# Transformer block on one core: shared-expert blocks reordered around the last second norm and the last router

## What is computed

```python
x = x + tanh(g0) * attention(layernorm(x), ctx)      # scores, softmax, values, output projection
h = layernorm(x)                                     # the second norm
router = h @ gate_w.T                                # 8 experts
top_p, top_i = top_k(softmax(router), 2)             # "ranking": the two best per token
y = sum over the two experts of top_p * ((silu(h @ fc1.T) * (h @ fc2.T)) @ proj.T)
shared = (silu(h @ sfc1.T) * (h @ sfc2.T)) @ sproj.T # 704 hidden units, for all tokens
y = y + sigmoid(h @ shared_gate_w.T) * shared
out = x + tanh(g1) * y
```

## Time and profile before

| | us |
|---|---|
| median of three runs | 304.88 |
| the profiled execution | 305.98 |
| its span, first to last instruction | 304.2 |
| PE busy | 276.9 (91%) |
| DVE busy | 215.7 (71%) |
| ACT busy | 170.6 (56%) |
| POOL busy | 131.1 (43%) |

### The profile page before, as it was taken

One profiled execution on the slowest core, in us unless ns is written; L12 is line 12 of the kernel. 1 busy time (PEld: TensorE's weight loads), 2 busy tenths in 40 slices (PEclk: granted clock), 3 DMA queues, 4 the chain that ended last, 5 costly groups with the idle time before them and its releaser, 6 DMA issues.

```text
span 304.2 us, 5865 instructions
## 1 busy us (share of the span) xinstructions
PE 276.9 (91%) x1785; PEld 249.0 (82%) x1785; DVE 215.7 (71%) x698; ACT 170.6 (56%) x399; POOL 131.1 (43%) x163
## 2 busy tenths in 40 slices
PE   0978989999999789799999999799999999999992
PEld 1867968888788667489888888689999999998891
DVE  2664777879968948766776775877787777863285
ACT  1565676777756546555325455456667666664230
POOL 1350361361587154732333000037777777786000
PEclk9997999999999999999999999999999999999996
DMA  6451107203028031433233665258888888866796
GB/s 196 173 176 69 70 11 239 82 21 122 1 77 280 1 110 53 151 130 120 92 123 128 188 232 185 59 134 139 136 136 138 137 137 143 126 71 69 239 353 239
DMA packets 30510, 40.18 MB, mean 132 GB/s; under 512 B 2960, under 2 KB 26640, under 8 KB 30480
## 3 DMA queue, kind: packets, MB, share of 16 engines
q1 hardware_dynamic: 22336, 29.53, 31.0%
q0 software_dynamic: 7152, 9.57, 19.0%
q10 hardware_dynamic: 992, 0.71, 0.9%
HBM read 22.68 MB, written 17.11 MB: 131 GB/s over the span
## 4 chain that ended last, share of the span: by engine, by line
PE 55%; DVE 23%; ACT 8%; issue 6%; POOL 3%; DMA 3%; DVEq 0%; ACTq 0%; SPq 0%; POOLq 0%
PE bank L415 43%; PE bank L654 6%; DVE ew_lo L1002 4%; ACT ew_hi L769 3%; PE bank L747 3%; DVE work L1332 3%; PE bank L703 3%; DVE xt_lo L1002 2%; ACT sh_hi L769 2%; DMA consts_sb<-consts_dram 2%; DVE work L1354 2%; DVE neg_max L1046 2%; ACT work L801 1%; DVE sh_lo L1002 1%; DMA weight_stage<-ew_dram 1%
## 5 line engine op out<-in xcount | busy, mean ns | idle before, releaser
L1522 POOL DMA_INDIRECT y_d<-work,dest_of_slot x39 | 60.5, 1552 | 56.3 <-DVE dest_of_slot L1378 54.7
L415 PE MATMUL bank<-ew_hi,xt_hi 128*128 (+2 forms) x172 | 53.8, 322 | 1.1 <-DVE xt_lo L1002 0.8
L415 PE MATMUL bank<-ew_lo,xt_hi 128*128 (+2 forms) x172 | 51.9, 302 | 0.0
L415 PE MATMUL bank<-ew_hi,xt_lo 128*128 (+1 forms) x133 | 40.5, 305 | 0.0
L1002 DVE TENSOR_TENSOR xt_lo<-bank,xt_hi 128x256 fp32r<-128x256 f32 (+2 forms) x90 | 35.7, 398 | 3.0 <-ACT xt_hi L769 1.5
L1482 POOL DMA_INDIRECT xs_d<-xn_all,slot_of_pair x32 | 32.0, 1001 | 10.1 <-issue 7.3
L415 PE MATMUL bank<-ew_hi 128*128 128x256 f32 (+1 forms) x100 | 31.5, 321 | 3.9 <-DVE ew_lo L1002 2.0
L1002 DVE TENSOR_TENSOR ew_lo<-bank,ew_hi 128x512 fp32r<-128x512 f32 (+1 forms) x41 | 22.7, 581 | 16.9 <-ACT ew_hi L769 16.8
L769 ACT ACTIVATE xt_hi<-bank 128x256 fp32r<-128x256 f32 (+1 forms) x90 | 32.7, 409 | 3.5 <-PE bank L747 2.2
L415 PE MATMUL bank<-xt_hi,sw_hi 128*128 128x512 f32 x88 | 34.6, 394 | 0.0
L415 PE MATMUL bank<-xt_lo,sw_hi 128*128 128x512 f32 x88 | 34.5, 392 | 0.0
(11 more groups left out here) (159 smaller groups left out, 688.5 us busy)
## 6 DMA issues: line engine op xcount, KB each, us to landing
work<-xs_d SPq DMA_DIRECT2D x39, 136.0 KB, 2.5
weight_stage<-ew_dram SPq DMA_DIRECT2D x10, 486.5 KB, 3.7
ew_hi<-y_d SPq DMA_DIRECT2D x8, 512.0 KB, 7.4
y_d<-work SPq DMA_DIRECT2D x6, 512.0 KB, 3.9
work<-ctx_t_dram SPq DMA_DIRECT2D x4, 512.0 KB, 3.5
xn_all<-x_dram SPq DMA_DIRECT2D x3, 512.0 KB, 6.5
xs_d<-pad_row SPq DMA_DIRECT2D x9, 136.0 KB, 1.8
weight_stage<-sw_dram SPq DMA_DIRECT2D x3, 384.0 KB, 3.2
```

What stands on the lines that cost most here:

```text
L415: last = nc.tensor.matmul(dst, a, b, start=(n == 0), stop=(n == len(pairs) - 1))
L1522: nc.gpsimd.indirect_dma_start(out=y2_d, out_offset=bass.IndirectOffsetOnAxis(ap=IX[:, n:n + 1], axis=0), in_=EY[:, n % 4, :], in_offset=None,
```

## The change

No instruction is added or removed: each engine has the same operations in another order.

- PE: the second half of `fc(0, 0)` goes ahead of `attend(3, 3)`. The first half stays behind it. The first half of `fc(0, 3)` goes ahead of `router(3)` and the second half between `router(3)` and `logits(3)`; before, the whole block stood behind `pj(0, 1)`. `route(3)` moves from behind `fc(0, 5)` to behind `pj(0, 4)`, and the wait for v_keep from behind `fc(1, 0)` to ahead of `fc(1, 1)`. The definition of `fc` moves up, and it gives its semaphore behind the half that is issued last.
- ACT: `second_apply(3, 1)` goes ahead of `s_hi(0, 0)`. Behind `logits(3)` comes `expert_weights(0)`, and then `s_hi(0, 2)`. `route_exp(3)` and the tanh of the shared gate move behind `s_hi(0, 3)`.
- DVE: `shared_tail_lo(1)` goes ahead of `s_lo(0, 0)`. `slots(2)`, `logits(3)` and `shifted(3)` stand behind `s_mult(0, 2)`, with `expert_weights(0)` after them and ahead of `s_lo(0, 2)`. `two_best(3)` goes behind `s_lo(0, 3)`, `counts(3)` behind `s_lo(0, 4)`, `shared_gate` behind `s_lo(0, 5)`.
- SP: the same list. The loads of pieces 0 and 1 still wait for the end of `shared_tail_lo(1)`, which uses the same staging buffer.

```diff
-PIECE_AT = ((0, 3), (0, 4), (1, 3), (1, 4), (1, 5), (2, 1), (2, 1), (2, 2), (2, 3), (2, 4))
+PIECE_AT = ((0, 2), (0, 4), (1, 3), (1, 4), (1, 5), (2, 1), (2, 1), (2, 2), (2, 3), (2, 4))
...
-                if halves[-1] == 1:
+                if halves[-1] == 1 and (s, j) != (0, 0) or (s, j, halves[0]) == (0, 0, 0):
                     last.then_inc(p_fc, 1)
...
                 if c < LAST:
                     project(c + 1, 3)
+                else:
+                    pe.wait_ge(sw_hi, 1)
+                    pe.wait_ge(sw_lo, 1)
+                    fc(0, 0, (1,))
                 attend(c, 3)
...
-            fc(0, 0)
+            fc(0, 0, (0,))
             fc(0, 1)
             route(LAST - 1)
             second_norm(LAST, 0)
             second_norm(LAST, 1)
             fc(0, 2)
+            fc(0, 3, (0,))
             router(LAST)
+            fc(0, 3, (1,))
             logits(LAST)
...
                     if n < len(order):
+                        if order[n] == (1, 0):
+                            route(LAST)
+                        if order[n] == (1, 1):
+                            pe.wait_ge(v_keep, 1)
                         fc(*order[n])
-                        if order[n] == (0, S_BLK - 1):
-                            route(LAST)
-                        if order[n] == (1, 0):
-                            pe.wait_ge(v_keep, 1)
...
             pj(0, 0)
-            blocks(0, PRE, 3)
+            pj(0, 1)
+            blocks(0, PRE, 4)
```

On ACT, in the loop over (s, j):

```diff
                     s_silu(s, j)
+                    if (s, j) == (0, 0):
+                        second_apply(LAST, 1)
+                    if (s, j) == (0, 1):
+                        second_hi(LAST, 0)
+                        second_hi(LAST, 1)
                     if (s, j) == (0, 2):
                         logits(LAST)
+                        expert_weights(0)
...
                     s_hi(s, j)
+                    if (s, j) == (0, 3):
                         route_exp(LAST)
                         act.wait_ge(v_lg, N_CH)
                         nc.scalar.activation(GS[:], LG[:, :, N_E], ACT.Tanh, scale=0.5).then_inc(a_gs, 1)
```

On DVE, in its loop:

```diff
-                    if (s, j) == (0, 2):
-                        logits(LAST)
-                        shifted(LAST)
                     s_mult(s, j)
+                    if (s, j) == (0, 0):
+                        shared_tail_lo(1)
                     if (s, j) == (0, 1):
                         second_lo(LAST, 0)
                         second_lo(LAST, 1)
+                    if (s, j) == (0, 2):
+                        slots(LAST - 1)
+                        logits(LAST)
+                        shifted(LAST)
+                        expert_weights(0)
...
                     s_lo(s, j)
-                    if (s, j) == (0, 0):
-                        slots(LAST - 1)
-                        shared_tail_lo(1)
-                    if (s, j) == (0, 2):
+                    if (s, j) == (0, 3):
                         two_best(LAST)
+                    if (s, j) == (0, 4):
                         counts(LAST)
+                    if (s, j) == (0, 5):
                         shared_gate()
-                    if (s, j) == (0, 5):
                         slots(LAST)
```

More of the change, by code:

```diff
@@ L566, in warm, with fc @@
                     nc.tensor.transpose(B[5][:, 0:P], ident, ident)
+            def fc(s, j, halves=(0, 1)):
+                for i in halves[:2 if j < S_FULL else 1]:
+                    last = chain(B[pair(s, j) + i][:],
+                                 [(SFC[a][:, k, 2 * j + i, :], XT[b][:, s, k, :]) for k in range(KD) for a, b in THREE],
+                                 [(0, v_h, 6 * s + j - 1)] if i == 0 else ())
+                if halves[-1] == 1 and (s, j) != (0, 0) or (s, j, halves[0]) == (0, 0, 0):
+                    last.then_inc(p_fc, 1)
             pe.wait_ge(d_const, 16)
@@ L624, in _ @@
                     project(c + 1, 3)
+                else:
+                    pe.wait_ge(sw_hi, 1)
+                    pe.wait_ge(sw_lo, 1)
+                    fc(0, 0, (1,))
                 attend(c, 3)
[L627 to L632, removed]
-                if halves[-1] == 1:
-                    last.then_inc(p_fc, 1)
             def pj(s, j):
@@ L965, in _ @@
                     s_silu(s, j)
+                    if (s, j) == (0, 0):
[3 more added lines that the diff above has]
+                        second_hi(LAST, 1)
                     if (s, j) == (0, 2):
                         logits(LAST)
+                        expert_weights(0)
+                    if (s, j) == (PRE - 1, S_FULL):
+                        e_step(-2, 2, -1)
+                    s_hi(s, j)
+                    if (s, j) == (0, 3):
                         route_exp(LAST)
@@ L970, in _ @@
                         nc.scalar.activation(GS[:], LG[:, :, N_E], ACT.Tanh, scale=0.5).then_inc(a_gs, 1)
[L971 to L976, removed]
-                    if (s, j) == (0, 0):
-                        second_apply(LAST, 1)
-                    for n in range(E_PIECES):
+                    for n in range(1, E_PIECES):
                         if PIECE_AT[n] == (s, j):
```

## The result

The changed kernel takes 301.65 us (median of 16 runs, 299.95 to 303.14), the kernel before in the same comparison 304.43 us (16 runs, 302.56 to 306.48). The ratio is 0.9898, 95% interval 0.9878 to 0.9918: faster by 2.8 us, about three times the 0.9 us that a measurement tells from no change. Forecast were 301.7 us and a gain of 3.2. That the time itself is met within 0.05 is luck: the gain is 0.4 smaller, and the kernel before took 0.45 less in this comparison than the 304.88 from which the forecast started.

What follows compares the result with a forecast made beforehand. The prediction took PE to bound the kernel, with DVE close behind. Filled waits gave 3.8 us at pj(0, 2), less 0.6 given back by DVE: a gain of 3.2, so 301.7 us, range 300.8 to 303.9.

Steps and rivals of the forecast that it cites:

- Step 1: PE, half of fc(0, 0) ahead of attend(3, 3): gain 1.38 us, hidden by a wait of 1.5; nothing held.
- Step 2: PE at second_norm(3, 1): the 1.26 us wait goes, as second_apply ends at 120.2; 0.10 is waited at route(2).
- Step 3: PE ahead of fc(0, 2): a new wait of 0.48 us for s_mult(0, 0) on DVE, bounds 0.3 and 0.7.
- Steps 4 and 5: PE at router(3) and logits(3): waits of 0.92 and 0.84 us go, with 0.45 and 0.4 to spare.
- Step 6: ACT's expert_weights(0) ahead of s_hi(0, 2), and pj(0, 2) directly behind pj(0, 1): costs nothing, up to 0.3 us.
- The sum: At pj(0, 2) on PE: 1.38 + 1.26 + 0.92 + 0.84 less 0.10 less 0.48, 3.8 us gained.
- Step 7: DVE up to s_mult(1, 0): counts(3) and the shared gate give back 0.6 us, bounds 0 and 1.25; 3.2 holds.
- Step 8: Exp and table loads behind s_hi(0, 3), then two_best ahead of s_mult(0, 4): costs nothing, with 0.4 us to spare.
- DVE holds more: Rival: late DVE blocks and the moved counts and gate cut the gain to 1.0 to 2.1 us; chance 0.17.
- Nothing is kept: Rival: expert weights, tables and scatters have a time of their own, so the time is 304.9 us; chance 0.09.
- the loop slows: Rival: expert loop steps take 0.09 us more, eating the 3.2, or 0.13 more, giving 306.5 us; chance 0.08.
- More is gained: Rival: counts and gate fall wholly into idle time and s_mult(0, 0) follows the attention, gain 3.9 to 4.2; chance 0.06.

Runs made afterwards that it cites:

- the last version: Changed kernel with counts(3) and shared gate in DVE's idle gaps and s_mult(0, 0) ahead of shared_tail_lo(0): 299.86 us, and 301.48 us on another chip.

## Why the prediction was right

- *Step 1* held exactly: the attention product's third matmul starts at 112.12, aligned 115.09, for the 115.10 of the earlier trace rows, and the next block where it was. Nothing is held.
- *Step 2*: the table load stands at 114.32, aligned 117.29 (said: 117.3), `second_apply` ends at 117.18, aligned 120.15 (120.2), `route(2)` waits 0.14 (0.10), the transposes run through.
- *Step 3*: `fc(0, 2)` starts at 118.66, aligned 121.63 (121.65). The new wait counted from the last transposes is only 0.25, and not 0.48, but the start is what enters the sum, and the difference is a drag in the small operations from `route(2)` on.
- *Steps 4 and 5*: the router at 122.87, aligned 125.84 (125.85), 0.74 to spare for 0.45; `logits(3)` without a wait, 0.9 to spare for 0.4. DVE was faster than my sum of its blocks by 0.3 to 0.5. The two runs that undo these edits bring the waits back.
- *Step 6*: ACT copies piece 0 at 124.96 with no wait for its load. `pj(0, 2)` starts at 129.06, aligned 132.03, for 131.98 (135.78 less 3.8); its lo part then costs 0.1, within the bound of 0.3.
- *The sum* of 3.8 is 3.75 there.
- *Step 7*: `s_mult(1, 0)` at 142.54, aligned 145.51, a gain of 2.94. DVE gives back 0.64 from `s_mult(0, 4)` (134.23, gained 3.58) on; said was 0.6. The run that moves both pieces into DVE's idle time brings 0.58 back in the stretch and 0.56 at `s_mult(1, 0)`, so these two pieces are the cause.
- *Step 8*: the exp ends at 132.04, aligned 135.0, 0.5 later than I had put it, and DVE waits 0.85 for it ahead of `two_best`. That ends just in time: `s_mult(0, 4)` still has 0.23 of idle time before it. The load again costs 1.28, and the exp follows 0.01 behind its end (130.52, 131.81). The drain that the Trainium skill gives in "ScalarE: Activation LUTs", section What ACT_TABLE_LOAD costs, doesn't appear in this trace either, and the gain of 2.2 by that rule didn't come.

The gain from there to the end is constant: 2.95 at `pj(1, 1)`, 2.93 at the span's end. What is missing from 3.2 is 0.05 in the sum at `pj(0, 2)`, 0.17 between there and `s_mult(0, 4)` (3.75 and 3.58; 0.1 of it is step 6's lo part, which had been put at nothing), and step 7's 0.64 for 0.6.

The rivals. *DVE holds more*: it holds 0.64, not over 1.25; its margins in steps 4 and 5 were wider than stated, that of step 8 narrower (0.23 for 0.4). *Nothing is kept* and *the loop slows*: the step is 2.00 and the gain at the loop's start is the gain at its end. *More is gained* needed two more moves on DVE: with them the stretch is 3.95 and 4.05 shorter than that of the kernel before.

What the prediction did not see is that its terms don't stand by themselves. It added 1.38, 1.26, 0.92 and 0.84 as if each belonged to an edit. In stretches:

```
whole change                                      +2.93
half block alone                                  -0.40
slots(2) later alone                              -1.34
taken back from the whole: half block              0.64 lost
                           slots(2)                1.17 lost
                           split of fc(0, 3)       2.70 lost
                           place of second_apply   3.46 lost
```

The four losses add up to 8.0, nearly three times the gain; by the ratios, which hold several executions each, they are about 0.3, 0.9, 2.3 and 2.6 us (in the order 0.9907, 0.9927, 0.9973, 0.9982 against 0.9898), 6.0 in all and still about twice the gain. Both single edits gain nothing by either measure (ratios 1.0017 and 1.001). The sum was right because I went along PE with all edits in place, not because four edits are worth four terms. Worked out edit by edit, from either side, it would have been wrong by microseconds.

## What to carry to other kernels

Take a reordering as one list: walk the engine that bounds with all edits in place, and ask at each wait who is late now. A part that fills one wait only lengthens the next unless the work behind that one comes earlier too, and a wait made longer can cost more than its length. Compare two traces from the last instruction ahead of the change, and leave out what differs before it.

## What the runs showed of the hardware

**The clock after a wait.** Between the start of the stretch and the expert loop the granted clock fell to 0.50 (the 1.2 GHz level) in three kernels and stood there for 3 to 4 us. In two it fell towards the end of a wait of PE of 2.39 us; in the third 1.8 us behind the end of a wait of 1.75 us, with one of 1.26 us 6.4 us earlier. It cost 1.3 to 1.5 us each time. In the kernel before, with waits of 1.26, 0.92 and 0.84 in these 8 us, and without the split with 0.64 and 1.33, it stayed at 1.00. I had not counted on this, and in the profiled executions it is over a third of what the norm at its old place loses, and all that `slots(2)` alone loses. All twelve profiled executions show a fall at the end too, within 3.1 us behind a wait of about 1.9 us ahead of PE's last product (292.91 in the changed kernel); it changes nothing between the kernels, since from that product to the span's end it is 5.3 to 5.4 us in each.

The wait just before doesn't decide alone. Ahead of the stretch, where the code is the same, the clock fell at 104 to 108 us in five of the twelve executions. The first line is the one with the half block taken back, the second the changed kernel again (columns as in the earlier trace rows):

```profile
104.00:108.00 4.00, 4.00 (x17) 3.22 (x16) 1.16 (x4) 1.20 (x5) 3.29 (x6) 0.57 0.54 192
104.00:108.00 4.00, 3.89 (x27) 3.23 (x28) 1.70 (x7) 1.80 (x6) 3.06 (x5) 1.00 0.49 171
```

PE is idle there for the same 0.7 and 0.5 us shortly before in all twelve. A fall cost 1.5: from the product behind the first of these waits to the last transposes it is 10.28 with it (101.80 to 112.08) and 8.75 without (101.47 to 110.22 in the changed kernel). The two executions with a fall at 122 are among the five. So the runs show neither a border between the waits, nor whether a single wait, their sum or something farther back decides; and that a wait of 2.39 at the norm brings the fall rests on two executions.

**The start.** The last transposes ahead of the change start at 110.2 to 113.2 us in the twelve profiled executions, whose code up to there does the same work. The windows of before, then of after, show the part that differs most (columns as in the earlier trace rows):

```profile
20.00:24.00 4.00, 2.09 (x13) 2.09 (x14) 1.87 (x4) 3.05 (x8) 0.00 (x0) 0.86 0.96 331
24.00:28.00 4.00, 3.41 (x21) 3.17 (x19) 1.27 (x3) 2.76 (x10) 0.00 (x0) 0.71 0.06 22
```

```profile
20.00:24.00 4.00, 3.94 (x32) 3.73 (x32) 1.75 (x5) 2.97 (x11) 0.00 (x0) 1.00 0.55 187
24.00:28.00 4.00, 2.14 (x12) 1.76 (x12) 2.40 (x4) 2.01 (x6) 0.00 (x0) 1.00 0.01 4
```

In before the loads run later (DMA share 0.96 there, 0.55 after), PE is half idle from 20 to 24 and the granted clock is 0.86 and then 0.71; after, PE is full and the clock stays at 1.00. The first transfer of the chain took 5.59 us in one (the constants) and 4.06 in the other (x), and 2.77 to 4.48 in the other runs. Why the loads differ was not tried.

The clock sorts the twelve. The two without a fall ahead of the stretch reach the transposes at 110.22 and 110.54; the eight with one fall, between 20 and 25 us or at 104, at 111.37 to 112.26; the one with two, the last version's second profile, at 112.64; and before, with a fall at 23 to 27 and the late loads, at 113.19. The times follow in the main: the five runs of the changed kernel with a mean granted clock of 0.995 or more took 299.95 to 301.22 us, the two at 0.981 or less 302.33 and 302.98 (the slowest, 303.14, had 0.986). So a median of a few runs also tells how many of them had a fall; it fits that the two medians of the last version (299.86 and 301.48) are 1.6 apart and its stretches 0.10. As large as the change's effect, the start is why the profiled spans (5.9 us apart) told twice what the medians do (2.8).
